# Token blocks of a layer kernel: running decay products in padded segments by one scan, a reciprocal for two products, two state operations a chunk

## What is computed

```
x = x + attention(layernorm(x));   x = x + ffn(layernorm(x))
q, k, v = heads of h @ Wq + bq, h @ Wk + bk, h @ Wv + bv       # 16 heads of D = 32
gate  = sigmoid(silu(h @ Wg1 + bg1) @ Wg2 + bg2);  alpha = 0.9*gate + 0.1
intra = causal softmax(q k^T / sqrt(D)) v                      # inside each chunk of 64 tokens
inter: for every token t:  out_t = q_t S;  S = alpha_t[:, None]*S + k_t v_t^T
attention = inter + intra
ffn   = shared expert (F 384) + top-8 of 64 experts, 256 slots each, weighted by router probabilities
```

## Time and profile before

| | |
|---|---|
| median of 3 runs | 5173.64 us (5163.59 to 5175.42) |
| the profiled execution | 5188.65 us; its span, first to last instruction, 5186.9 us |
| PE busy | 4629.1 us (89%) |
| DVE busy | 4004.0 us (77%) |
| ACT busy | 2260.5 us (44%) |
| POOL busy | 1161.5 us (22%) |
| mean granted TensorE clock | 0.953 of full speed |

### The profile page before, as it was taken

How to read it: one execution, slowest core, us unless ns; L and a number is a source line. 1 busy time by engine, 2 the same in 40 slices (tenths; PEclk the granted TensorE clock), 3 DMA queues, 4 the chain that set the end, 5 groups by cost and what they waited for, 6 DMA issues and landing times. The chain is left out here.

```text
span 5186.9 us, 184061 instructions
## 1 busy us (share of the span) xinstructions
PE 4629.1 (89%) x74544; PEld 4004.3 (77%) x74544; DVE 4004.0 (77%) x7960; ACT 2260.5 (44%) x7475; POOL 1161.5 (22%) x1077
## 2 busy tenths in 40 slices
PE   5889889988888889888998889889899978999998
PEld 5777777777777777777777777777777757999998
DVE  5777777777777777777777777777777768888887
ACT  3434333334343333433333333433333335666666
POOL 1111111111111111111111111111111125666666
PEclk9999999999999999999999999999998988999999
DMA  2000000000000000000000000000000027999997
GB/s 60 28 28 28 28 28 28 28 28 28 28 28 28 28 28 28 28 28 27 28 25 28 28 28 28 28 28 28 28 28 28 28 81 223 268 264 270 265 269 202
DMA packets 195055, 358.53 MB, mean 69 GB/s; under 512 B 16736, under 2 KB 92896, under 8 KB 194352
## 3 DMA queue, kind: packets, MB, share of 16 engines
q1 hardware_dynamic: 160848, 269.47, 15.3%
q0 software_dynamic: 33632, 79.73, 7.0%
HBM read 243.87 MB, written 107.50 MB: 68 GB/s over the span
## 5 line engine op out<-in xcount | busy, mean ns | idle before, releaser
L547 ACT ACTIVATE PR<-PR,MX 128x64 f32<-128x64 f32 x2048 | 683.5, 335 | 1257.1 <-DVE MX L1122 1257.1
L445 POOL TENSOR_TENSOR rs<-ve,neg_half 128x1 f32<-128x1 f32 x128 | 69.1, 540 | 3088.4 <-DVE ve L1156 3088.4
L1074 DVE RECIPROCAL AL<-AL 128x256 f32<-128x256 f32 x260 | 453.8, 1745 | 0.1
L685 PE MATMUL bank<-XTh,wsguh 128*128 128x256 f32 x1536 | 445.2, 290 | 0.0
L1616 PE MATMUL ebank<-XH,WH 128*128 128x256 f32 x1536 | 430.8, 280 | 7.4 <-DVE XL L1698 7.4
L686 PE MATMUL bank<-XTl,wsguh 128*128 128x256 f32 x1536 | 436.7, 284 | 0.0
L687 PE MATMUL bank<-XTh,wsgul 128*128 128x256 f32 x1536 | 435.5, 283 | 0.0
L1616 PE MATMUL ebank<-XH,WL 128*128 128x256 f32 x1536 | 429.4, 280 | 0.0
L1616 PE MATMUL ebank<-XL,WH 128*128 128x256 f32 x1536 | 429.4, 280 | 0.0
L1143 DVE TENSOR_TENSOR WT<-pt_bank,AM 128x512 f32<-128x512 f32 x256 | 177.1, 692 | 301.1 <-PE pt_bank L822 301.1
L1691 DVE TENSOR_TENSOR WL<-WS,WH 128x768 fp32r<-128x768 f32 (+1 forms) x455 | 371.3, 841 | 20.7 <-issue 4.5
(11 more groups left out here) (224 smaller groups left out, 14028.2 us busy)
## 6 DMA issues: line engine op xcount, KB each, us to landing
WS<-in_L_ffn_w_gate_dram SPq DMA_DIRECT2D x65, 768.0 KB
WS<-in_L_ffn_w_up_dram SPq DMA_DIRECT2D x65, 768.0 KB
WS<-in_L_ffn_w_down_dram SPq DMA_DIRECT2D x65, 768.0 KB
norm_rows<-XR SPq DMA_DIRECT2D x64, 576.0 KB, 3.6
X<-in_L_attn_x_dram SPq DMA_DIRECT2D x66, 512.0 KB, 3.6
out_dram<-X SPq DMA_DIRECT2D x64, 512.0 KB, 3.9
CR<-token_counts,count_at POOLq DMA_INDIRECT x136
XG<-norm_rows,row_at POOLq DMA_INDIRECT x132
```

The costliest lines, as they stand in the source:

```text
L445: nc.gpsimd.tensor_tensor(rs2[:, k:k + 1], ve2[:, k:k + 1], neg_half[:, k:k + 1], ALU.pow).then_inc(rstd2_ready.sem, 1)
L547: ins = nc.scalar.activation(PR[b][:, j, :], PR[b][:, j, :], ACT.Exp, bias=MX[b][:, j:j + 1], scale=1.0, accum_out=SU[b][:, j:j + 1])
L685: nc.tensor.matmul(out, sh, mh, start=first, stop=False)
L1074: ins = v.reciprocal(AL[:, m, :], AL[:, m, :])
```

## The change

It does four things. (1) AL gets one extra column per segment of 32 tokens (`PAD` = 33): the column in front holds 0, alpha goes into the other 32. One scan over 264 columns instead of 256 then leaves 1, A_1, ..., A_32 in each segment, so columns 0 to 31 are E and columns 1 to 32 are A, in one tensor; EX, its copy and the multiply go. (2) The reciprocals are taken of PV, the products A_i times A_(33-i), 16 for each segment of 32, so there are two `inverse` calls of 128x256 instead of four; 1/A_i is then PV's reciprocal times A_(33-i), which two multiplies on POOL (`unpair`) write to RI, reading one operand backwards. The two calls `inverse`(n, 2) and `inverse`(n, 3), which stood around `norm1`(t+2), are gone. (3) The corrections of the first half-chunks are made on the factors (`fold` on POOL: a small r_mid, then RI's and AL's first halves) and no longer on KD and QD, which are one multiply each. (4) The state chain multiplies U straight into the next chunk's R by FX = end factor times next mid factor, so S is written only at the block's end.

```diff
+NS = TB // HC
+PAD = HC + 1
...
-        stages = [QT[0], QT[1], KT[0], KT[1], QD, KD, V, X2, KTok, AL, EX]
+        stages = [QT[0], QT[1], KT[0], KT[1], QD, KD, V, X2, KTok, RI, XN]
...
+            def unpair(t):
+
+                pool.wait_ge(inverted.sem, t.value(inverted))
+                pool.wait_ge(kd_ready.sem, t.value(kd_ready, back=1))
+                apart(pool, pool_apart)
+                nc.gpsimd.tensor_tensor(inverse[:, :, 0:half], PV[:, :, :], running[:, :, HC:half:-1],
+                                        ALU.mult).then_inc(folded.sem, 1)
+                nc.gpsimd.tensor_tensor(inverse[:, :, half:HC], PV[:, :, ::-1], running[:, :, half:0:-1],
+                                        ALU.mult).then_inc(folded.sem, 1)
+
+            def fold(t):
+
+                pool.wait_ge(qd_ready.sem, t.value(qd_ready, back=1))
+                nc.gpsimd.tensor_tensor(r_mid[:, :].unsqueeze(2), halves(PV[:, :, 0:1]), halves(running[:, :, 1:2]),
+                                        ALU.mult).then_inc(folded.sem, 1)
+                pool.wait_ge(folded.sem, t.value(folded, 1))
+                m = FS[t.buf][:, :, :, 0].rearrange("p c n -> p (c n)")
+                first = halves(inverse)
+                nc.gpsimd.tensor_tensor(first, first, bc(m, HC), ALU.mult).then_inc(folded.sem, 1)
+                pool.wait_ge(folded.sem, t.value(folded, 2))
+                first = halves(running[:, :, 0:HC])
+                nc.gpsimd.tensor_tensor(first, first, bc(r_mid[:, :], HC), ALU.mult).then_inc(folded.sem, 1)
...
                     for k in range(NT):
                         rstd2(t, k)
+                    unpair(t.next())
                     rstd1(t.next(2))
+                    fold(t.next())
                     decayed_k(t.next())
                     decayed_q(t.next())
...
                 dve.wait_ge(g1_tanh.sem, t.value(g1_tanh))
                 dve.wait_ge(g2_filled.sem, t.value(g2_filled, back=1))
+                dve.wait_ge(qd_ready.sem, t.value(qd_ready, back=1))
+                link(v.memset(running[:, :, 0:1], 0.0))
                 v.scalar_tensor_tensor(s1[:, :], t1[:, :], 1.0, z1[:, :], ALU.add, ALU.mult).then_inc(s1_ready.sem, 1)
...
                 dve.wait_ge(al_ready.sem, t.value(al_ready))
+                for m in range(KC):
+                    ins = v.tensor_tensor_scan(AL[:, m, :], AL[:, m, :], seg_start[:, :], 0.0, ALU.mult, ALU.add)
+                link(ins)
+
+            def products(t):
+                v.tensor_copy(FS[t.buf][:, :, :, :].rearrange("p c n a -> p (c n a)"), running[:, :, HC]).then_inc(fs_ready.sem, 1)
                 dve.wait_ge(qd_ready.sem, t.value(qd_ready, back=1))
-                v.memset(segs(EX[:, :, :])[:, :, 0:1], 0.0)
-                link(v.tensor_copy(segs(EX[:, :, :])[:, :, 1:HC], segs(AL[:, :, :])[:, :, 0:HC - 1]))
-                for m in range(KC):
-                    ins = v.tensor_tensor_scan(EX[:, m, :], EX[:, m, :], seg_start[:, :], 0.0, ALU.mult, ALU.add)
-                link(ins)
-                link(v.tensor_tensor(AL[:, :, :], EX[:, :, :], AL[:, :, :], ALU.mult))
...
+                v.tensor_tensor(PV[:, :, :], running[:, :, 1:HC // 2 + 1], running[:, :, HC:HC // 2:-1], ALU.mult)
                 dve.wait_ge(fs_ready.sem, t.value(fs_ready))
+                link(v.tensor_tensor(FX[t.buf][:, :, :], FS[t.buf][:, :, 0:NCH - 1, 1], FS[t.buf][:, :, 1:NCH, 0], ALU.mult))
...
                     norm2(t, 1)
                     values(n, 1)
                     x2t_low(t)
-                    inverse(n, 2)
                     norm1(t.next(2))
-                    inverse(n, 3)
                     hidden(t, 0)
```

More of the change, by code:

```diff
@@ L164, in phase_tokens @@
         s1 = sb("s1", [GP, TB])
-        AL = sb("AL", [P, KC, TB])
-        EX = sb("EX", [P, KC, TB])
+        AL = sb("AL", [P, KC, NS * PAD])
+        PV = sb("PV", [P, KC * NS, HC // 2])
+        RI = sb("RI", [P, KC, TB])
+        r_mid = sb("r_mid", [P, KC * NCH])
         QT = [sb(f"QT{i}", [P, KC, TB]) for i in range(2)]
@@ L171, in phase_tokens @@
         FS = [sb(f"FS{i}", [P, KC, NCH, 2]) for i in range(2)]
+        FX = [sb(f"FX{i}", [P, KC, NCH - 1]) for i in range(2)]
         V = sb("V", [P, NT, DIM])
@@ L431, in _ @@
             link(nc.gpsimd.memset(seg_start[:, :], 0.0))
-            link(nc.gpsimd.memset(seg_start[:, :].rearrange("p (s t) -> p s t", t=HC)[:, :, 0:1], 1.0))
+            link(nc.gpsimd.memset(seg_start[:, :].rearrange("p (s t) -> p s t", t=PAD)[:, :, 0:1], 1.0))
             link(nc.gpsimd.memset(keep[:, :], 1.0))
@@ L450, in bc, with halves @@
                 return ap.unsqueeze(2).to_broadcast([ap.shape[0], ap.shape[1], n])
+            running = AL[:, :, :].rearrange("p c (s t) -> p (c s) t", t=PAD)
+            inverse = RI[:, :, :].rearrange("p c (s t) -> p (c s) t", t=HC)
+            half = HC // 2
+            def halves(ap):
+                return ap.rearrange("p (n a) t -> p n a t", a=2)[:, :, 0, :]
+            def unpair(t):
[6 more added lines that the diff above has]
+                                        ALU.mult).then_inc(folded.sem, 1)
@@ L459, in decayed_q @@
[L459 to L463, removed]
+                nc.gpsimd.tensor_tensor(split(QD[:, :, :]), split(QT[t.buf][:, :, :]), running[:, :, 0:HC],
+                                        ALU.mult).then_inc(qd_ready.sem, 1)
@@ L471, in decayed_k @@
                 apart(pool, pool_apart)
[L472 to L477, removed]
+                nc.gpsimd.tensor_tensor(KD[:, :, :], KT[t.buf][:, :, :], RI[:, :, :], ALU.mult).then_inc(kd_ready.sem, 1)
             rstd1(Turn(0, 0))
+            unpair(Turn(0, 0))
+            fold(Turn(0, 0))
+            decayed_k(Turn(0, 0))
             decayed_q(Turn(0, 0))
-            decayed_k(Turn(0, 0))
             rstd1(Turn(0, 1))
@@ L528, in alpha @@
                 act.wait_ge(th_ready.sem, t.value(th_ready))
-                nc.scalar.activation(AL[:, :, :], AL[:, :, :], ACT.Copy, bias=0.55, scale=0.45).then_inc(al_ready.sem, 1)
+                kept = AL[:, :, :].rearrange("p c (s t) -> p (c s) t", t=PAD)[:, :, 1:PAD]
+                nc.scalar.activation(kept, kept, ACT.Copy, bias=0.55, scale=0.45).then_inc(al_ready.sem, 1)
             def qk_evac(t, k, filled, ready, dst, bias, scale, names):
@@ L1009, in _ @@
         def _(dve):
-            LINKS = 39
+            LINKS = 34
             links = [0, None]
@@ L1059, in decays, with inverse @@
                 dve.wait_ge(al_ready.sem, t.value(al_ready))
[L1060 to L1075 removed]
+                for m in range(KC):
[3 more added lines that the diff above has]
+                v.tensor_copy(FS[t.buf][:, :, :, :].rearrange("p c n a -> p (c n a)"), running[:, :, HC]).then_inc(fs_ready.sem, 1)
+                dve.wait_ge(qd_ready.sem, t.value(qd_ready, back=1))
+                v.tensor_tensor(PV[:, :, :], running[:, :, 1:HC // 2 + 1], running[:, :, HC:HC // 2:-1], ALU.mult)
+                dve.wait_ge(fs_ready.sem, t.value(fs_ready))
+                link(v.tensor_tensor(FX[t.buf][:, :, :], FS[t.buf][:, :, 0:NCH - 1, 1], FS[t.buf][:, :, 1:NCH, 0], ALU.mult))
+            def inverse(t, k):
+                part = PV[:, k * (KC * NS // 2):(k + 1) * (KC * NS // 2), :]
+                ins = v.reciprocal(part, part)
+                if k == 1:
                     ins.then_inc(inverted.sem, 1)
@@ L1242, in _ @@
             v.memset(ends[:, :], 0.0)
+            v.memset(AL[:, :, :], 0.0)
             v.memset(S[:, :, :], 0.0).then_inc(consts_done, 1)
@@ L1262, in _ @@
             products(t)
-            for m in range(KC):
-                inverse(t, m)
+            for k in range(2):
+                inverse(t, k)
             for k in range(NT):
```

37 lines of the change are left out of this document (16 added, 21 removed).

## The result

The changed kernel takes 5198.13 us (median of 20 runs), the kernel before 5169.27 us (20 runs) beside it. The ratio is 1.0049 [1.0037, 1.0061]: **slower by some 25 us**, where +47 us was forecast. The direction and the holds of XR and of HTl or sh came out as forecast, the size at about half, and an effect of TensorE's clock had been priced at nothing.

What follows compares the result with a forecast made beforehand. PE's in-order waits for the softmax division, XR, XTl and XN were taken to bound each block, not DVE's total work. 64 x (-0.9 + 0.1 + 1.6) - 4 = +47 us gave 5221 us, range 5125 to 5285 us.

Steps and rivals of the forecast that it cites:

- C: XR on DVE is held by POOL's first `unpair` multiply: +0.9 us on the path to XTl and the router.
- D: XN: HTl and sh wait for POOL's multiplies, so `hidden`(1) starts late; +1.6 us for PE's `xt`, C included.
- Clock: Granted clock: C makes the low stretch at the router more frequent; priced at 0.
- A: In front of unit 2's softmax division: DVE's work 0.94 us less, PE's 0.86 us wait closes; -0.9 us a block.
- B: `silu1`: a memset of 32 and its wait stand in front of s1, which PE takes at once; +0.1 us.
- E: Two reciprocals and three state operations a block, beside other work on DVE: nothing gained beyond A.
- F: Prologue: DVE's part is shorter, XN of the second block follows earlier; -4 us, once.
- The sign that I named: Sign of D: PE's wait for XN in all blocks and over 1.5 us each.
- A new clock fall: Rival: PE's pause before XN's transposes grows and brings clock falls, 0.8 us a block; 5272 us; chance 0.12.
- XR is let through first: Rival: XR issues before POOL's multiply, C is 0, D +0.7; 5164 us, no measurable change; chance 0.14.
- The slow POOL patterns: Rival: POOL slower on backward 16-element patterns, a half costs 2.40 us; a block +2.1, 5304 us; chance 0.09.

Runs made afterwards that it cites:

- XR first: The changed kernel, with POOL's first `unpair` multiply waiting for XR of tile 1: 5149.22 us, ratio 0.9945 to the kernel before.
- unpair between: The changed kernel, with `unpair` between `rstd2`'s two powers and no wait added: 5151.71 us, ratio 0.9933 to the kernel before.
- the control: The kernel before, with two unused POOL multiplies of 512 on constants added behind a wait for XR: 5175.9 us, ratio 0.9987.
- the run with the memset moved: The changed kernel, with the memset of the padding columns moved out of `silu1`, behind the last chunk's `state`: 5195.75 us, ratio 1.0032.
- unpair late: The changed kernel, with `unpair` behind `rstd1` on POOL and nothing waiting for XR: 5172.53 us, ratio 0.999 to the kernel before.
- folds-early kernel: The changed kernel, with POOL's list as wait for XR, `unpair`, both folds, then `rstd1`, KD, QD: 5072.5 us, ratio 0.9792.

## Why the prediction was right in direction and too large in size

- **C, XR held: right.** Forecast 0.9 us more; XR of tile 1 went from 0.55 to 1.41 us on the mean, +0.86. The rule of the Trainium skill ("SBUF — State Buffer", Who interferes with whom), that the one that issues first keeps the shared ports for the whole instruction, gave the same, and the runs agree with it: XR first, unpair between and the control move nothing but the order of issue.
- **D, XN later: the holds are as forecast, but that +1.51 comes so near +1.6 is part luck.** Two errors of opposite sign stand in it. In the 45 blocks in which POOL holds HTl or sh, `xt` comes 18.96 us behind the residual, +1.33 and not +1.6: `unpair`'s halves took 1.20 and 1.39, r_mid 0.24 and QD 2.21, where I had taken 0.3 for r_mid and 2.37 for QD, and QD ends 15.85 us behind the residual where my sum gives 16.1. That is 17 us too much. In the other 18 blocks `hidden`(1) waits for its tanh and not for POOL, and they bring the mean to 19.14: 0.18 us a block, 12 us, which I had at nothing (see Clock). Together D is 6 us too large. That `hidden`(1) starts at the same time whether HTl goes between KD and QD or behind QD held, to 0.3 us.
- **A: the step that failed.** I said that DVE's part gets 0.94 us shorter and that PE "waits 0.86 us there, so the wait closes: -0.9 us a block". Measured is -1.11, which is 64 x 0.21 = 13 us of the 18 by which the sum below shrinks. The mechanism held, the wait closed; its size was wrong. Two things were wrong. The idle time in the earlier trace rows counts from the modelled end of the last matmul (2118.39 + 0.40), but the next instruction needn't wait for that end: matmuls there start each 0.23 us. By the starts the pause was 1.26 - 0.23 = 1.03 us. And DVE saved 1.24 us, not 0.94: from AM's start to the division's it now takes 4.27 us, before 5.51. FX starts 0.61 us behind PV where I had taken 0.72, and PV starts only 0.10 behind the FS copy. Behind the new division DVE is 0.12 us ahead of PE, so PE now sets the place, at 1.24 - 0.12 = 1.12. That is more than the pause of 1.03, because the matmuls just ahead of it come sooner too (0.10 us in one block compared row by row).
- **B, the memset: too small by half.** +0.1 forecast. It was put between 0 and 0.19; 0.125 by the wait for s, 0.20 by the run with the memset moved. Net of the state chain's 0.07 it is +0.13 in three of every four blocks. The row of the table is +0.25, because every fourth block has more, 11.68 us before and 12.28 here. PE's program is a loop of four blocks a turn, and its waits with the releaser "issue" at L836 (26.0 us in 13 blocks of 52) are there; they stand in the kernel before too (23.8 us). The runs with the same instructions in this stretch scatter between 11.8 and 12.3 us in that block, so this rest of 0.12 us a block is not shown to be of the change.
- **E, the reciprocals, right; the state operations, 0.07 us a block and not 0.** 5.5 us a block off DVE gave nothing else beyond A: the stretches between the marks other than those of A, C, D and B moved by 0.05 us at most, the last one left out for the clock.
- **F, the prologue: -5 us and not -4.**
- **Clock: the other step that failed.** I wrote that C makes the fall at the router more frequent and priced that at 0, since in the kernel before XN comes at the same time in blocks with and without it. That was so there: `hidden`(1) waits for its tanh in 28 of 63 blocks and starts at 14.85, and is held in 35 and starts at 14.84. In the changed kernel the clock granted from 4 to 12 us behind the residual falls from 0.90 to 0.75, and where it is 0.57 `hidden`(1) starts with its tanh, 0.65 us later than in the blocks that POOL holds (16.81 against 16.16). With XR first, where the clock there is 0.88, no such block is left. This is shown for the distance from residual to `xt` only: those 18 blocks as a whole are no longer than the others (65.2 and 65.5 us), since the falls behind them differ too. PE waits for XN in 36 of the blocks, 0.73 us each, and not in all of them for over 1.5 us as I wrote: with the lower clock PE itself comes later to XN's transposes. The sign that I named was wrong in form; XN's own start, +1.51 us behind the residual (16.07 to 17.58), contains the clock as well.

By this the forecast's +47 us becomes 47 - 13 (A) - 6 (D) - 1 (F) + 2 (B) = +29 us, against 25 to 29 measured. The agreement is closer than the working: the 8 us of every fourth block and the -6 us of the stretches that I called unchanged are not in it and nearly cancel.

None of the rivals took place as written. "A new clock fall" did in part: the lower clock came at the router, where it costs 0.18 us a block, and not behind XN's pause, where 0.8 was feared. The next was "XR is let through first", which hung on 0.08 us: it stayed on the side that the row of before had shown, in all blocks. The slow POOL patterns did not come: 1.20 us backwards in rows of 16, the upper end of what I had allowed for a half; a plain multiply of 512 on constants takes 1.04.

## What to carry to other kernels

Where POOL multiplies run beside DVE, ask of each DVE operation on the critical path which POOL operation is issued just ahead of it; the fix took no instruction more than a wait: putting a POOL multiply in a gap in which POOL waits anyway, or behind the critical DVE operation, was worth 2.6% here. Shortening an engine's total work is worth only the pause that it closes: 5.5 us a block off DVE gave 1.1 and 0.07. Before taking a wait as the one that sets the time, count in how many blocks it does: a mean over blocks of different forms (16.20 us in the run with `unpair` late) can be a time that no block has. And measure a pause of PE from start to start, less the spacing of the matmuls ahead of it, not by the idle time in the row.

## What the runs showed of the hardware that was not expected

- A waiting DVE operation gets in between two POOL operations that follow each other at once, but the next one is issued too late for the same gap: behind HTl, which got in between KD and QD, sh is issued when QD has begun and is held for 2.15 us (unpair late). The POOL operation behind such a gap takes longer: the second `unpair` half 1.39 us behind the held XR and 1.21 where XR ran first, QD 2.38 us in the unpair-late kernel behind HTl and 2.20 in the folds-early kernel, and of two equal multiplies on constants the second, behind the held XR, 1.23 us where both take 1.04 in the control. So it is 0.18 us each time; why wasn't tried.
- A multiply of 512 on POOL takes 1.20 us read backwards in rows of 16 (the first `unpair` half reads one operand so, the second both), 1.04 plain on constants, and 1.06 in place with a factor repeated over 32 elements. QD, which reads rows of 33, took 2.21 us, KD with plain rows 2.39; why the first is shorter wasn't tried.
- A held DVE operation's row begins where it was issued and has the wait in its duration. DVE's busy time thus contains waiting: in the changed kernel, 0.86 us a block of XR alone.
